# Values of the context in five blocks, and six reorderings, in a fused attention and mixture-of-experts kernel

## The chip, the cores and the metric

One Trainium2 chip, one core of it. The metric is the device time of one execution in microseconds (us). The kernel before takes 1630.91 us, the median of 3 runs (1629.7 to 1631.23). Engines: PE is the matrix engine (TensorE), DVE the vector engine, ACT the scalar engine, POOL the GpSimd engine; SP only issues DMAs. Each runs its own instruction stream in order and waits on semaphores.

## The reference

```python
def _L0_xattn_ref(queries, keys, values, Wq, bq, Wk, bk, Wv, bv, Wo, bo):   # 8 sequences, 512 rows, 77 context rows
    q = (queries @ Wq + bq).reshape(B, L, 16, 32)
    k = (keys @ Wk + bk).reshape(B, S, 16, 32)
    v = (values @ Wv + bv).reshape(B, S, 16, 32)
    scores = jnp.einsum('blhd,bshd->bhls', q, k)
    scores = jnp.where(causal[None, None], -jnp.inf, scores)      # triu, k=1
    attn = jax.nn.softmax(scores * scale, axis=-1)
    return jnp.einsum('bhls,bshd->blhd', attn, v).reshape(B, L, 512) @ Wo + bo

def _L0_ffn_ref(hidden_states, ...):      # attention runs over axis 0: the 8 sequences, causal, for each of 512 places
    ln1 = _layer_norm(hidden_states, ln1_weight, ln1_bias)
    ... q, k, v from ln1 @ qkv_weight.T (16 heads, 4 groups of keys), scores, softmax, proj ...
    h1 = hidden_states + proj
    x = _layer_norm(h1, ln2_weight, ln2_bias).reshape(-1, 512)
    probs = softmax(x @ router_weight)             # 8 experts, each token takes its best 2
    # each expert takes at most 1280 tokens, in order
    fc1 = jax.nn.gelu(jnp.einsum('ech,ehf->ecf', xt, moe_w1))
    fc2 = jnp.einsum('ecf,efh->ech', fc1, moe_w2)
    return h1 + (scatter-add of fc2 * padded_probs)
x = x + _L0_xattn_ref(_layernorm(x), ctx_1024, ctx_1024, ...)
x = x + _L0_ffn_ref(_layernorm(x), ...)
```

The 4096 rows are 32 tiles of 128. Weights and activations are float32; the large products are made as three passes of a high and a low half.

## The kernel before

There are two parts. The first (`build_main`) is a software pipeline of 52 steps written out by hand: in step i each engine does one stage of several tiles. With t a tile of the first attention and f a block of 128 tokens of the second, `tile(i, lag)` is the tile that is `lag` behind step i, and FF = 14 is where the second attention begins.

In step i PE does, in this order: the transposes of the normalized rows of tile i-1 ("xt"), the transposes of the probabilities of tile i-4 ("pt", four banks, L1010), those of the second attention ("p2t"), the transposes of z, the normalized block i-14 ("zt", L971, after waiting for `z_done`), in even steps the queries of two tiles (48 matmuls, L355), the output projection of tile i-5 ("wo", 12 matmuls), the second attention's scores and output ("s2", "o2"), the scores of tile i-2 ("s", L1060, into banks 0 to 3), the second attention's products (L1074) with the router's logits between them (L1079), for tiles 0 to 7 the values of one sequence ("val", L1091: 77 rows, 4 matmuls of 512 columns into bank 4 or 5), the transposes of the router's input ("z2t", L971 too), the product with the values of tile i-4 ("pv", L1103), the second projection ("pj"), and last, in steps 47 to 49 and 51, the prefix counts of the routing (`count_places`, L983 to L987).

DVE adds the causal mask to the scores of tiles 0 to 7 (L887), takes the row maximum (L888), subtracts it in two halves (L898), then adds the bias to the values (L918) straight into `va`, then forms the low halves of the attention's output (`oT_lo`, L821, wanted by wo) and of the transposed rows (`xT_lo`, L827, wanted by the queries), statistics, the sums of the exponentials (L952) and, last of a step, z (L959). In steps up to 14 ACT makes the exponentials of a tile in the next step, from then on in the same step; it normalizes x (`norm_x`, L563) before that in steps below 14 and after that from 14 on. POOL computes the factors of the normalizations, multiplies probabilities by their reciprocal sums (L482), and forms some low halves.

A PSUM bank is given out by `psum_plan`. Below step 14 each kind has banks of its own; from 14 on the jobs of a step take turns in banks 0 to 3 (half 0) and 4 to 7 (half 1), and a job waits until the readers of its bank's last user are done (`bank_free`). The scores always take banks 0 to 3. wo is in half 0.

The routing's choice of experts is made by `choose` on DVE: ten dependent small instructions for a batch of blocks, with 27 blocks in step 46, 4 in step 50 and the last one alone.

The second part (`build_experts`) goes over 8 experts by 5 groups of 256 tokens, 40 groups in all; a group whose first row is past the table has no tokens, and PE skips its matmuls. PE in a step: first layer of group i-6 (L1403, 96 matmuls), transposes of the gathered rows of group i-4 (L1416), second layer of group i-7 (L1432, 48 matmuls). POOL in a step: the gather of group i-3 (two indirect DMAs, L1292), the low halves of the next expert's weights (`low`, L1204), the scatter of group i-7 (two indirect DMAs, L1303). DVE makes `og`, the weighed result (L1372), which waits for the scatter of the group before; PE's second layer waits for `og` of the group before.

Of the kernel before, what the change touches and what calls it, by code (L numbers as in the profile page):

```python
# [18 lines left out]
ALU = mybir.AluOpType  # L19
# [147 lines left out]
CHOICES = ((STEPS - 6, 0, 27), (STEPS - 2, 27, 31), (STEPS, 31, 32))  # L167
COUNTS = {STEPS - 5: (0, 7, 1), STEPS - 4: (7, 15, 1), STEPS - 3: (15, 27, 1), STEPS - 1: (27, 31, 2)}
# [8 lines left out]
def psum_jobs(i):  # L177
# [8 lines left out]
    if tq is not None and tq < S:  # L186
        jobs += [("val", tq, 0, 1)]
# [4 lines left out]
def own_bank(kind, t, j):  # L192

    if kind == "q":
        return j
    if kind in ("pt", "val"):
        return 4 + j % 2
    odd = {"xt": t, "pv": t + LP - 1, "wo": t + LP + 1}[kind] % 2
    return 6 + odd


def psum_plan():
# [11 lines left out]
    for i in range(STEPS):  # L214
# [3 lines left out]
        for kind, t, j, half in psum_jobs(i):  # L218
            if i < FF and kind != "s":
# [9 lines left out]
def build_main(nc, a, x2d, mid, out2d, z2d, small, logits, tops, choice, row_table, weights, groups, sb, sem):  # L229
# [49 lines left out]
    bv = vbd[0:SK, :, :, :].rearrange("p g j d -> p (g j d)")  # L279
# [11 lines left out]
    gap, ex = sb("gap", [P, 1]), sb("ex", [P, 2])  # L291
# [6 lines left out]
    with main_psum:  # L298
# [18 lines left out]
        const_in = sem("const_in")  # L317
        place, ousted = psum_plan()
# [42 lines left out]

        def weight_piece(i):
# [19 lines left out]
        def _(sp):  # L382
# [19 lines left out]
            for i in range(STEPS):  # L402
                if 0 < i < NT - 2:
                    load_x(i + 2)
                t = tile(i, LP)
# [20 lines left out]
                if f is not None:  # L426
                    for n in range(2):
                        sp.wait_ge(x2_out[n], 16 * 4 * (f // 8 + 1))
                    sp.wait_ge(s["piece_lo"], 8)
                    need(sp, base_out[f % FX], 64 * (f // FX))  # L430
# [16 lines left out]
        def _(pool):  # L447
# [28 lines left out]
            for i in range(STEPS):  # L476
# [26 lines left out]
                if f is not None:  # L503
                    pool.wait_ge(s["v_kept"], f + 1)
                    pool.wait_ge(s["val_done"], S)
# [7 lines left out]
                if t is not None:  # L513
                    pool.wait_ge(bias_in, 32)
                    pool.wait_ge(xc_in[t % 2], 16 * (t // 2 + 1))
                    pool.tensor_tensor(xc[:, t % 2, :], xc[:, t % 2, :], bo[:, :], ALU.add).then_inc(s["bias_x"], 1)
                t = tile(i, -1)
# [11 lines left out]
                if i <= LATE:  # L529
                    factors(i)  # L530
# [18 lines left out]
                if i == 11:  # L549
                    pool.wait_ge(s["val_mm"], S)  # L550
# [9 lines left out]
        def _(act):  # L560
# [29 lines left out]
            act.dma_start(bv, a["L0_xattn_bv"].partition_broadcast(SK)).then_inc(bias_in, 16)  # L590
            act.dma_start(bo[:, :], a["L0_xattn_bo"].partition_broadcast(P)).then_inc(bias_in, 16)
            for i in range(STEPS):
# [27 lines left out]
                f = tile(i, FF)  # L620
                if f is not None:
                    act.wait_ge(s["zt_mm"], f + 1)
                    act.wait_ge(s["val_mm"], S)
                    need(act, s["z_lo"], f)
                    for k in range(KT):
# [878 lines left out]
```

## Time and profile before

| | |
|---|---|
| median of 3 runs | 1630.91 us |
| the profiled execution's own time | 1629.14 us |
| its span, first to last instruction | 1627.3 us |
| PE busy | 1517.0 us, 93% |
| DVE busy | 919.9 us, 57% |
| POOL busy | 839.5 us, 52% |
| ACT busy | 712.0 us, 44% |
| mean granted clock of PE | 0.964 of full speed |

PE is busy for 93% of the span, so the 110 us in which it isn't, and those in which its clock is lowered, are where reordering can act; beside it, only less PE work helps. In the page's forty slices PE's digit is 8 or 9 nearly everywhere, with lows at slice 21 (5), the passage between the two parts, at slice 32 (7), and at the end (6). The granted clock has its lows at slices 20 and 21.

### The profile page before, as it was taken

How to read it: one execution, taken by the hardware profiler on the slowest of the kernel's cores; microseconds unless marked ns; L12 is line 12 of the kernel's file. 1: busy time of each engine (PE TensorE's matmuls, PEld its weight loads, DVE VectorE, ACT ScalarE, POOL GpSimd, SP SyncE). 2: the span in 40 equal slices, each digit the busy share in tenths (PEclk: the TensorE clock that was granted, in tenths of full speed). 3: DMA queues.
4: the chain of work that ended last, by engine and by line, in shares of the span. 5: the costliest groups of instructions: out<-in, count | busy, mean ns of one | idle time of the engine just before them, and what ended most of it. 6: DMA issues, size and time to landing. Idle time of an engine off the chain costs nothing. (4 is left out here: it accounts for less than half of the span.)

```text
span 1627.3 us, 31053 instructions
## 1 busy us (share of the span) xinstructions
PE 1517.0 (93%) x11103; PEld 1326.0 (81%) x11104; DVE 919.9 (57%) x1719; ACT 712.0 (44%) x1425; POOL 839.5 (52%) x953
## 2 busy tenths in 40 slices
PE   7899889999999999999858999999999789999986
PEld 5577778888888888788648897998999689999976
DVE  3657457777777767787665455432333744343361
ACT  2445445555555555466315344432333633343351
POOL 2444444666556655688544566632533846454242
PEclk9999889999999999999968999999999989999999
DMA  6112111122212112122223233433422523442121
GB/s 247 47 48 72 57 64 50 64 79 73 71 68 85 58 56 78 64 88 89 82 72 102 59 94 94 113 77 72 91 67 50 126 66 93 100 104 50 29 39 24
DMA packets 63595, 124.57 MB, mean 77 GB/s; under 512 B 13231, under 2 KB 13647, under 8 KB 62920
## 3 DMA queue, kind: packets, MB, share of 16 engines
q1 hardware_dynamic: 45184, 92.54, 17.3%
q0 software_dynamic: 17920, 29.31, 10.3%
q8 instruction: 108, 1.77, 0.5%
q10 hardware_dynamic: 328, 0.50, 0.1%
q14 instruction: 55, 0.45, 0.1%
HBM read 89.02 MB, written 46.27 MB: 83 GB/s over the span
## 5 line engine op out<-in xcount | busy, mean ns | idle before, releaser
L1403 PE MATMUL hidden_ps<-gT,w 128*128 128x256 f32 x2880 | 356.1, 286 | 9.2 <-issue 6.0
L1403 PEld LDWEIGHTS hidden_ps<-gT,w 128*128 128x128 f32 x2880 | 353.6, 193 | 13.2 <-issue 7.6
L1432 PE MATMUL expert_ps<-w,hT 128*128 128x512 f32 x1440 | 342.4, 398 | 8.1 <-DVE og L1372 8.1
L1432 PEld LDWEIGHTS expert_ps<-w,hT 128*128 128x128 f32 x1440 | 272.9, 191 | 66.1 <-DVE og L1372 8.5
L1204 POOL TENSOR_TENSOR w<-raw,w 128x1024 fp32r<-128x1024 f32 x64 | 155.0, 2434 | 248.0 <-ACT w L1198 247.9
L1347 DVE TENSOR_TENSOR hT<-gl,hT 128x512 fp32r<-128x512 f32 x160 | 130.5, 824 | 259.4 <-ACT hT L1322 259.4
L1320 ACT ACTIVATE gl<-hidden_ps 128x512 f32<-128x512 f32 x160 | 95.7, 598 | 342.3 <-PE hidden_ps L1403 320.2
L1303 POOL DMA_INDIRECT out_dram<-og,idx x80 | 129.7, 1621 | 107.6 <-DVE og L1372 79.6
L1372 DVE TENSOR_SCALAR og<-expert_ps,kept 128x512 f32<-128x512 f32 x80 | 59.1, 749 | 157.7 <-PE expert_ps L1432 157.3
L1330 ACT ACTIVATE gT<-yk 128x256 fp32r<-128x256 f32 x160 | 66.9, 418 | 125.3 <-DVE yk L1358 123.9
L1292 POOL DMA_INDIRECT xg<-normed_tokens,idx x80 | 91.5, 1144 | 48.0 <-POOL idx L1287 33.6
L1074 PE MATMUL main_ps<-wqkv_hi,zT 128*128 128x512 f32 x256 | 108.9, 441 | 2.5 <-DVE h L851 2.5
L1322 ACT ACTIVATE hT<-hidden_ps 128x512 fp32r<-128x512 f32 x160 | 95.3, 596 | 15.1 <-PE expert_ps L1432 15.1
L864 DVE TENSOR_TENSOR x<-main_ps,xc 128x512 f32<-128x512 f32 x32 | 22.1, 691 | 122.9 <-PE main_ps L355 122.9
L1358 DVE TENSOR_SCALAR yk<-gather_ps,small 128x256 f32<-128x256 f32 x160 | 83.1, 540 | 2.9
L482 POOL TENSOR_TENSOR pr<-pr,rec 128x616 f32<-128x616 f32 x64 | 77.5, 1232 | 2.0 <-DVE rec L953 1.8
L355 PE MATMUL main_ps<-xT_hi,wq_hi 128*128 128x256 f32 x256 | 75.4, 295 | 2.9 <-DVE xT_lo L827 2.9
L1010 PE MATMUL main_ps<-small,pr 128*77 128x128 f32 x512 | 67.8, 285 | 11.0 <-ACT pT L610 5.5
L610 ACT ACTIVATE pT<-main_ps 77x512 f32<-77x512 f32 x128 | 67.1, 593 | 18.2 <-PE main_ps L1010 18.1
L355 PE MATMUL main_ps<-xT_lo,wq_hi 128*128 128x256 f32 x256 | 73.5, 287 | 0.0
L355 PE MATMUL main_ps<-xT_hi,wq_lo 128*128 128x256 f32 x256 | 73.5, 287 | 0.0
L1010 PEld LDWEIGHTS main_ps<-small,pr 128*77 128x77 f32 x512 | 60.4, 155 | 15.8 <-issue 14.8
(179 smaller groups left out, 3121.1 us busy)
## 6 DMA issues: line engine op xcount, KB each, us to landing
raw<-L_ffn_moe_w_dram SPq DMA_DIRECT2D x64, 512.0 KB, 3.6
normed_tokens<-h SPq DMA_DIRECT2D x128, 65.0 KB
xa<-x_dram SPq DMA_DIRECT2D x32, 256.0 KB, 2.7
xc<-x_dram SPq DMA_DIRECT2D x32, 256.0 KB, 3.0
attended_rows<-x SPq DMA_DIRECT2D x32, 256.0 KB, 2.2
fx<-attended_rows SPq DMA_DIRECT2D x128, 64.0 KB
out_dram<-fx SPq DMA_DIRECT2D x128, 64.0 KB
fx<-qkv_rows_dram SPq DMA_DIRECT2D x1, 1536.0 KB, 6.8
```

The costliest lines, as they stand in the source:

```text
L355: last = pe.matmul(dst, lhs(l, k), rhs(r, k), start=k == 0 and n == 0, stop=k == KT - 1 and n == 2)
L1010: last = pe.transpose(bank("pt", tp, b)[0:SK, g * P:(g + 1) * P], pr[:, tp % 2, b, g, :], ident)
L1074: last = pe.matmul(bank("qkv", fq, 0), zT[fq % 2][l][:, k, :], wqkv[r][:, k, 0:D], start=k == 0 and n == 0, stop=k == KT - 1 and n == 2)
L1204: pool.tensor_tensor(weight_piece(p, 1, j), raw[:, j % 2, :], weight_piece(p, 0, j).bitcast(F32), ALU.subtract).then_inc(s["w_lo"], 1)
L1292: pool.indirect_dma_start(out=xg[:, g.s % 2, k, :], out_offset=None, in_=z2d[:, :], in_offset=rows(g, k), bounds_check=N - 1, oob_is_err=F ...
L1303: pool.indirect_dma_start(out=out2d[:, :], out_offset=rows(g, k), in_=og[:, k, :], in_offset=None, bounds_check=N - 1, oob_is_err=False, c ...
L1320: act.activation(gl[:, q % 2, :], pH[:, q, :], ACT.Gelu_apprx_tanh)
L1322: act.activation(hT[g.s % 2][0][:, 2 * q:2 * q + 2, :].rearrange("p f n -> p (f n)"), pH[:, q, :], ACT.Gelu_apprx_tanh).then_inc(s["gelu"], 1)
L1347: dve.tensor_tensor(o[1], gl[:, q % 2, :], o[0].bitcast(F32), ALU.subtract)\
L1358: dve.tensor_scalar(yk[:, k % 2, :].rearrange("p (b n) -> p b n", b=GB), pT[:, :, k * P:(k + 1) * P], ln2w[:, k:k + 1], ln2b[:, k:k + 1], ...
L1403: last = pe.matmul(pH[:, q, f * W:(f + 1) * W], w1[p][l][:, k, cols], xT[g.s % 2][r][:, k, :], start=k == 0 and n == 0, stop=k == KT - 1 a ...
L1432: last = pe.matmul(pY[:, k, :], hT[par][l][:, f, k * P:(k + 1) * P], w2[p][r][:, f, :], start=f == 0 and n == 0, stop=f == FT - 1 and n == 2)
```

## The change

Five blocks of values. All 616 context rows are taken as 5 blocks of 128 rows (the last has 104) instead of 8 sequences of 77. Block b is computed in step b+2, ahead of the scores, and gets its bias on DVE into a staging tile (`fx[6]`), ahead of the scores' mask and maximum; SP then moves its rows to their sequences in `va` by two or three DMAs.

Order in the first part. zt goes behind the queries on PE, and its copies go behind the copies of q on ACT; wo's bank comes from half 1 instead of half 0; step 14 still uses the kinds' own banks; ACT's `norm_x` stays early up to step 15; DVE makes z ahead of the exponentials' sums in steps 13 and 14, POOL its factors earlier up to step 14.

Routing. The first batch of the choice is split in three of 9 (steps 42, 44, 46); the counts are spread over steps 47 to 51 and stand ahead of the scores' place in PE's step; `gap` has two columns.

Experts. POOL's order becomes gather (i-3), scatter (i-8), low halves: each scatter now comes behind the next gather. PE's first layer waits for the gathered rows quarter by quarter.

```diff
-CHOICES = ((STEPS - 6, 0, 27), (STEPS - 2, 27, 31), (STEPS, 31, 32))
-COUNTS = {STEPS - 5: (0, 7, 1), STEPS - 4: (7, 15, 1), STEPS - 3: (15, 27, 1), STEPS - 1: (27, 31, 2)}
+VB = -(-S * SK // P)
+CHOICES = ((STEPS - 10, 0, 9), (STEPS - 8, 9, 18), (STEPS - 6, 18, 27), (STEPS - 2, 27, 31), (STEPS, 31, 32))
+COUNTS = {STEPS - 5: (0, 6, 1), STEPS - 4: (6, 13, 2), STEPS - 3: (13, 21, 3), STEPS - 2: (21, 27, 3),
+          STEPS - 1: (27, 31, 4)}
...
-    jobs = [("xt", tx, 0, 1)] + [("pt", tp, j, 0) for j in range(4)] + [("p2t", fo, 0, 0), ("zt", fz, 0, 0)]
+    jobs = [("xt", tx, 0, 1)] + [("pt", tp, j, 0) for j in range(4)] + [("p2t", fo, 0, 0)]
...
-    jobs += [("wo", tw, 0, 0), ("s2", fs, 0, 1), ("o2", fo, 0, 1), ("s", tq, 0, 0), ("qkv", fq, 0, 1),
+    jobs += [("zt", fz, 0, 0), ("wo", tw, 0, 1), ("s2", fs, 0, 1), ("o2", fo, 0, 1)]
+    if 0 <= i - 2 < VB:
+        jobs += [("val", i - 2, 0, 1)]
+    jobs += [("s", tq, 0, 0), ("qkv", fq, 0, 1),
...
-            if i < FF and kind != "s":
+            if i <= FF and kind != "s":
...
+                b = i - 3
+                if 0 <= b < VB:
+                    sp.wait_ge(s["val_done"], b + 1)
+                    for seq, row, key, n in value_rows(b):
+                        sp.dma_start(va[key:key + n, seq, :, :].rearrange("p h d -> p (h d)"), stage[row:row + n, :])\
+                          .then_inc(va_in[b], 16)
...
+                b = i - 2
+                if 0 <= b < VB:
+                    dve.wait_ge(s["val_mm"], b + 1)
+                    dve.wait_ge(bias_in, 32)
+                    if b > 0:
+                        dve.wait_ge(va_in[b - 1], 16 * len(value_rows(b - 1)))
+                    n = min(P, S * SK - P * b)
+                    dve.tensor_tensor(stage[0:n, :], bank("val", b)[0:n, :], bv[0:n, :], ALU.add)\
+                       .then_inc(s["val_done"], 1)
...
-                if t is not None and t > 1 and i < FF:
+                if t is not None and t > 1 and i < FF + 2:
                     norm_x(t)
...
-                if fz is not None:
-                    pe.wait_ge(s["z_done"], fz + 1)
-                    transposes("zt", fz, z).then_inc(s["zt_mm"], 1)
                 if i % 2 == 0 and tq is not None:
...
+                if fz is not None:
+                    pe.wait_ge(s["z_done"], fz + 1)
+                    transposes("zt", fz, z).then_inc(s["zt_mm"], 1)
...
+                if i in COUNTS:
+                    count_places(*COUNTS[i])
+                b = i - 2
+                if 0 <= b < VB:
+                    pe.wait_ge(wv_in, 16)
+                    bank_free(pe, "val", b)
+                    n = min(P, S * SK - P * b)
+                    for k in range(KT):
+                        last = pe.matmul(bank("val", b)[0:n, :], cT[:, k, P * b:P * b + n], rv[:, k, :],
+                                         start=k == 0, stop=k == KT - 1)
+                    last.then_inc(s["val_mm"], 1)
...
-                    need(pe, s["val_done"], min(tp + 1, S))
+                    if tp < S:
+                        for b in range(tp * SK // P, (tp * SK + SK - 1) // P + 1):
+                            pe.wait_ge(va_in[b], 16 * len(value_rows(b)))
...
-                for piece in split_pieces(c, i):
-                    low(pool, *piece)
-                g = At(c, i - 7, PER)
+                g = At(c, i - 8, PER)
                 if g.within(NG):
...
+                for piece in split_pieces(c, i):
+                    low(pool, *piece)
...
-                    pe.wait_ge(s["xt_lo"], g.count(KT, KT))
+                    pe.wait_ge(s["xt_lo"], g.count(KT, 1))
...
+                                    if q == 0 and f == 0:
+                                        pe.wait_ge(s["xt_lo"], g.count(KT, k + 1))
```

## Rows read from the trace of the kernel before

**Rows 1.** Busy time by stretch: PE, PEld, DVE, ACT, POOL, clock, DMA share, GB/s.
```profile
280.00:640.00 360.00, 359.72 (x3155) 313.84 (x3154) 266.62 (x522) 199.14 (x439) 219.08 (x335) 1.00 0.21 69
```

**Rows 2.** Timeline of PE, steps 4 to 6: start, us, instruction, [idle before <-releaser].
```profile
60.73 1.13 PE L1060 MATMUL main_ps<-kT,qT 32*128 32x77 f32 x32 [1.24 <-ACT qT L638]
...
73.83 3.66 PE L1091 MATMUL main_ps<-ctx_then_block 128*77 128x512 f32 x8
...
81.87 0.37 PE L355 MATMUL main_ps<-xT_hi,wq_hi 128*128 128x256 f32 x1
...
90.50 1.13 PE L1060 MATMUL main_ps<-kT,qT 32*128 32x77 f32 x32
```

**Rows 3.** Timeline of DVE, step 5.
```profile
73.96 1.45 DVE L887 TENSOR_TENSOR main_ps<-main_ps,small 128x1232 f32<-128x1232 f32 x1
...
78.35 0.68 DVE L918 TENSOR_TENSOR va<-main_ps,vbd 77x512 f32<-77x512 f32 x1
79.19 0.69 DVE L821 TENSOR_TENSOR oT_lo<-main_ps,oT_hi 128x512 fp32r<-128x512 f32 x1 [0.17 <-ACT oT_hi L586]
```

**Rows 4.** The DMA issues: count, KB each, median us from issue to landing.
```profile
attended_rows<-x SPq DMA_DIRECT2D x32, 256.0 KB, 2.2
...
xg<-normed_tokens,idx POOLq DMA_INDIRECT x80, 3.6
out_dram<-og,idx POOLq DMA_INDIRECT x80, 5.7
```

**Rows 5.** Timeline of PE, steps 13 to 16.
```profile
179.59 1.13 PE L1060 MATMUL main_ps<-kT,qT 32*128 32x77 f32 x32
...
183.91 3.00 PE L1010 MATMUL main_ps<-small,pr 128*77 128x128 f32 x16 [1.60 <-DVE pr L898]
191.16 1.11 PE L971 MATMUL main_ps<-small,ctx_then_block 128*128 128x128 f32 x4 [4.24 <-DVE ctx_then_block L959]
...
202.77 1.13 PE L1060 MATMUL main_ps<-kT,qT 32*128 32x77 f32 x32 [0.88 <-DVE x L864]
...
208.45 1.12 PE L971 MATMUL main_ps<-small,xa 128*128 128x128 f32 x4 [3.54 <-ACT xa L563]
...
216.82 1.13 PE L1060 MATMUL main_ps<-kT,qT 32*128 32x77 f32 x32 [1.09 <-DVE x L864]
...
229.51 0.58 PE L355 MATMUL main_ps<-xT_hi,wq_hi 128*128 128x256 f32 x1 [0.66 <-DVE xT_lo L827]
```

**Rows 6.** Timeline of DVE, step 13.
```profile
185.07 0.68 DVE L827 TENSOR_TENSOR xT_lo<-main_ps,xT_hi 128x512 fp32r<-128x512 f32 x1
```

**Rows 7.** Timeline of DVE, the choice in steps 46 and 50.
```profile
778.39 0.38 DVE L732 TENSOR_TENSOR equal<-logits,tops 128x216 f32<-128x216 f32 x1
...
781.77 2.00 DVE L735 TENSOR_TENSOR hot<-first,consts 128x216 f32<-128x216 f32 x1
...
823.05 0.18 DVE L732 TENSOR_TENSOR equal<-logits,tops 128x32 f32<-128x32 f32 x1
```

**Rows 8.** Timeline of PE, steps 46 to 50.
```profile
785.08 0.52 PE L1074 MATMUL main_ps<-wqkv_hi,zT 128*128 128x512 f32 x1 [2.48 <-DVE h L851]
...
801.26 0.66 PE L971 MATMUL main_ps<-small,h 128*128 128x128 f32 x4 [2.38 <-DVE h L906]
...
822.92 1.11 PE L971 MATMUL main_ps<-small,h 128*128 128x128 f32 x4 [2.55 <-DVE h L906]
...
827.05 1.04 PE L1079 MATMUL main_ps<-small,ctx_then_block 128*128 128x8 f32 x8
```

**Rows 9.** Timeline of PE at its longest wait among the experts.
```profile
1301.87 1.09 PE L1416 MATMUL gather_ps<-small,xg 128*128 128x128 f32 x4 [8.73 <-DMA xg<-normed_tokens,idx]
```

**Rows 10.** Timeline of POOL ahead of that wait.
```profile
1293.41 1.89 POOL L1303 DMA_INDIRECT out_dram<-og,idx  x1 [0.16 <-issue]
...
1298.24 1.09 POOL L1292 DMA_INDIRECT xg<-normed_tokens,idx  x1 [0.88 <-POOL idx L1287]
```

**Rows 11.** Timeline of DVE in the same stretch.
```profile
1299.47 1.41 DVE L1372 TENSOR_SCALAR og<-expert_ps,kept 128x512 f32<-128x512 f32 x2
```

More of the change, by code:

```diff
@@ L317, in build_main @@
         const_in = sem("const_in")
+        va_in = [sem(f"va_in{b}") for b in range(VB)]
         place, ousted = psum_plan()
@@ L360, in parts, with value_rows @@
             return ap.rearrange("p (k n) -> p k n", k=KT)
+        def value_rows(b):
+            found = []
+            for seq in range(S):
+                first, end = max(seq * SK, P * b), min((seq + 1) * SK, P * (b + 1))
+                if first < end:
+                    found.append((seq, first - P * b, first - seq * SK, end - first))
+            return found
         def weight_piece(i):
@@ L619, in _ @@
                     act.activation(p2T, parts(bank("p2t", f)), ACT.Copy).then_inc(s["p2t_evac"], 1)
[L620 to L625, printed above, removed]
-                        act.activation(y[:, k, :], bank("zt", f)[:, k * P:(k + 1) * P], ACT.Identity,
-                                       bias=ln1b[:, k:k + 1], scale=ln1w[:, k:k + 1]).then_inc(s["y_done"], 1)
-                    act.wait_ge(s["y_done"], 4 * f + 4)
-                    need(act, s["qkv_mm"], 2 * (f - 1))
-                    act.activation(zT[f % 2][0][:, :, :], y, ACT.Copy).then_inc(s["z_hi"], 1)
                 if i % 2 == 0 and tile(i, 2) is not None:
@@ L639, in _ @@
                                        ACT.Identity, bias=bq[:, m:m + 1]).then_inc(s["q_evac"], 1)
+                f = tile(i, FF)
+                if f is not None:
+                    act.wait_ge(s["zt_mm"], f + 1)
+                    act.wait_ge(s["val_mm"], VB)
+                    need(act, s["z_lo"], f)
+                    for k in range(KT):
+                        act.activation(y[:, k, :], bank("zt", f)[:, k * P:(k + 1) * P], ACT.Identity,
+                                       bias=ln1b[:, k:k + 1], scale=ln1w[:, k:k + 1]).then_inc(s["y_done"], 1)
+                    act.wait_ge(s["y_done"], 4 * f + 4)
+                    need(act, s["qkv_mm"], 2 * (f - 1))
+                    act.activation(zT[f % 2][0][:, :, :], y, ACT.Copy).then_inc(s["z_hi"], 1)
                 t = tile(i, 0)
-                if t is not None and t > 1 and i < FF:
+                if t is not None and t > 1 and i < FF + 2:
                     norm_x(t)
@@ L673, in _ @@
                 t = tile(i, 0)
-                if t is not None and i >= FF:
+                if t is not None and i >= FF + 2:
                     norm_x(t)
@@ L688, in _ @@
                     need(act, s["weighed"], f - 1)
[L689 removed]
+                    act.activation(ex[:, f % 2:f % 2 + 1], gap[:, f % 2:f % 2 + 1], ACT.Exp).then_inc(s["gap_exp"], 1)
                 piece = weight_piece(i)
@@ L1086, in _ @@
                                   lambda h, k: wqkv[h][:, k, D:QKV]).then_inc(s["qkv_mm"], 1)
-                if tq is not None and tq < S:
-                    pe.wait_ge(wv_in, 16)
-                    bank_free(pe, "val", tq)
-                    for k in range(KT):
-                        last = pe.matmul(bank("val", tq)[0:SK, :], cT[:, k, tq * SK:(tq + 1) * SK], rv[:, k, :],
-                                         start=k == 0, stop=k == KT - 1)
-                    last.then_inc(s["val_mm"], 1)
                 if ft is not None:
```

55 lines of the change are left out of this document (29 added, 26 removed).

## The prediction

> **What bounds the kernel now.** First the busy shares: PE works 93% of the span, the others 44 to 57%. Then the same by stretch. From 280 to 640 us PE is busy for 359.72 of 360 us [rows 1]: in the steady steps nothing but less PE work can help, and the change takes none away there. So the question is what it does in the four places where PE isn't full: the steps that make values (2 to 9, up to 138 us), the steps where the second attention starts (13 to 17), the last steps of the first part (46 to 51), and the short steps among the experts. For each I read the timeline of PE for its waits, and of the engine named as releaser for what it had been doing.
>
> **Values in five blocks.** The four matmuls of a step's values take 3.66 us, 3.6 without the overlap with what follows [rows 2]; their length goes by the 512 columns, not by 77 or 128 rows, so five steps cost what five of the eight did: 3 x 3.6 = 10.8 us less PE work. That is not the gain. Before, the values stand behind the scores and cover DVE's work on them. From the values' end (73.83 + 3.66 = 77.49) to the queries at 81.87 PE has 4.4 us of other work [rows 2]. DVE starts on the scores at 73.96, is through mask, maximum and subtraction at 78.35 (4.4 us), and then forms oT_lo (0.6 to the next start) and xT_lo (0.7) [rows 3, 6]. In the new order, with no values behind the scores, wo may start 4.4 + 0.7 + 0.1 = 5.2 us after the scores' end and the queries 5.8 us after it, while PE is ready after 4.4: it waits 0.8 us in an odd and 1.4 us in an even step. The mask is there for tiles 0 to 7, so this holds at the passages into steps 5 to 10: 3 x (0.8 + 1.4) = 6.6 us given back. (From step 10 on there is no mask, and the order there is as before.) At the start the values, now between queries and scores, fill the 1.24 us in which PE waits for the copy of q in step 4 [rows 2], and the bias comes off DVE's queue ahead of the subtraction (0.68 us [rows 3]), which frees the banks of the next transposes; I take 2.2 us for both (bounds 1.2 and 3.6, the cover of one values step). Term 1: -10.8 + 6.6 - 2.2 = -6.4 us; bounds -13 (all of it PE's) and -2.
>
> The added DMAs cost nothing in the sum. SP issues a block's two or three in the step after its bias; DMAs of rows land 2.2 us after issue, and the extremes of that view are 2.2 and 5.7 [rows 4]. Their first reader is the product with the values, last in a PE step of 10 to 18 us; the other is DVE's next bias, which waits behind the queries and wo (8.6 us [rows 2]) in an even step. Behind SP's new wait stand only the loads of xc, wanted a step later. With that cover gone, four blocks (all but the first) would cost 2.2 us each. The wider bias load is one DMA at the start.
>
> **Steps 13 to 17.** The scores of step 13 end at 180.7 [rows 5]. PE then waits for a bank (1.60) and for z (4.24), and starts the queries at 191.16 + 0.76 = 191.9 [rows 5]. With step 14 on its own banks and zt behind the queries, what ends last is xT_lo, 185.07 + 0.68 = 185.8 [rows 6]: 6.1 us gained. z goes 0.7 us behind that, long before the queries (5.7 us) are over. Queries and wo took 191.9 to 201.9 = 10.0 us here against 81.87 to 90.50 = 8.6 us in step 6 [rows 2, 5]: they ran after 5.8 us of waits, at a lowered clock for part of it, so with waits under 1 us I take 1.4 us as gained (bounds 0 and 1.4). The scores' wait of 0.88 for DVE x goes with wo's bank; so does that of 1.09 in step 15 [rows 5]. zt adds 4 transposes behind the queries, 0.6 us, where they stood in a stall's shadow; in step 16 once more. In step 15 the wait of 3.54 for ACT's normalization [rows 5] goes too, but I count nothing for it: wo there hangs on oT_lo, which DVE reaches after maximum, subtraction, statistics, sums and z, all behind the same scores. In step 16 it is the same: the queries come 229.51 - 217.95 = 11.6 us after the scores [rows 5] by DVE's queue, whichever way zt is put. Term 2: -6.1 - 1.4 - 0.9 - 1.1 + 0.6 + 0.6 = -8.3 us; bounds -13 and -4. From step 17 on, zero: q goes ahead of y on ACT, and the scores, which now wait for y too in even steps, come 5.7 us (wo, s2, o2) behind zt, while y takes about 2.5. POOL's low half of z comes later in even steps, but the queue behind it waits for o2 anyway.
>
> **Choice.** The batch of 27 blocks runs from 778.39 until DVE h can release PE at 785.08: ten instructions of 0.38 us on 216 elements, one of which took 2.00 [rows 7]. PE waits 2.48 us for it [rows 8]. On 32 elements one takes 0.18 us [rows 7]; for 72 I take 0.23, with the gap between two 2.7 us for a batch. In step 46 DVE is then 3.1 us earlier, and the wait and (an estimate, from step 14's) 1.3 us of lower clock behind it are gone: -3.8. In steps 42 and 44 2.7 us are added to DVE, which has some idle time but is followed closely by PE: bounds 0 and 2.7 for each, I take 0.9. Term 3: -3.8 + 1.8 = -2.0 us; bounds -3.8 and +1.6.
>
> The 2.00 us instruction runs while POOL forms a low half of a weight. [...] It speaks against this change: the added batches run in steps where POOL is busier. If each met one such hold of 1.6 us, the sum would be 3.2 us smaller, and the time some 1610.
>
> **Counts.** From 822.92 + 1.1 to 827.05 the counts of 12 blocks stand on PE between two links of the routing's chain: 3.0 us, 0.25 a block [rows 8]. Put ahead of the logits they fall into waits of 2.38 and 2.55 us [rows 8]. Gained: 7 x 0.25 = 1.7 us in step 47; nothing in step 48, whose successor hangs on DVE and POOL behind pj; 1.5 us before the last logits, where six blocks' counts and the copies of y2 (1.5 us) now run together. Filled waits should also keep the clock up: 1.5 us, between 0 and 3. Term 4: -4.7 us; bounds -6 and -2.
>
> **Experts.** The longest wait, 8.73 us, is for a gather [rows 9]. POOL is busy without a break ahead of it; the gather's issue at 1298.24 stands behind a scatter that began at 1293.41, two issues of 1.9 us [rows 10]. In the new order it is issued 3.8 us earlier. What is late next is the scatter, issued 4 us later: `og` at 1299.47 [rows 11] waits for it, landing up to 5.7 us after issue [rows 4], and the second layer for `og`. So of 3.8 us I take 2 (bounds 0 and 5, if one other wait shortens too). In full steps of 23 us both have room. The finer wait of the first layer gains nothing: those rows are two steps old. Term 5: -2 us.
>
> **Sum.** -6.4 - 8.3 - 2.0 - 4.7 - 2 = -23.4 us. The profiled execution took 1629.1 us, 1.8 above its span of 1627.3, and is itself 1.8 below the median of 1630.9; 1629.1 - 23.4 = 1605.7 us, and against the median 1607.5. I say 1607.
>
> **Rivals.**
> A. PE stays the bound where I see DVE take over. For it: PE's waits in steps 4 to 12 are under 1 us before. Against: the sum 4.4 + 0.7 + 0.7 above. It gives 6.6 us more: 1600. Chance 0.12.
> B. The staging tile becomes the wait: DVE's bias waits until the last block has left it, scores' work is queued behind it, and PE gets wo and queries later. For it: one tile, not two, and SP's wait in order. Against: 8.6 us of cover. Four blocks at 2.2 to 3.6 us: +9 to +14, 1616 to 1621. Chance 0.15.
> C. The reordering of zt moves a wait and ends none: DVE's queue sets steps 14 to 17 throughout. For it: steps 15 and 16 as read above. Against: xT_lo at 185.8. Term 2 falls to -1: 1614. Chance 0.10.
> D. Slower: the scatter, now behind the gather, gets onto PE's path through `og`. Each group that it hits costs up to 1298.24 - 1293.41 = 4.8 us; it decides from 23.4 / 4.8 = 5 of the 40 groups on. With ten hit: +48 - 21.4 = +27, 1658. Against: in full steps a scatter has about 8 us to land in before the next `og`. Chance 0.05.
> E. The rule on SBUF ports as above, 1610: 0.04. No change to speak of (within 0.2%, 3 us, about what this kernel's measurement can tell): 0.02.
>
> The forecast keeps 0.52. From 1597 to 1619 about 8 in 10 are held. Faster 0.93, within 0.2% 0.02, slower 0.05.
>
> **What would show it.** The profile after should have 40 records of value matmuls at about 18 us; waits of about 1 us before wo and the queries in steps 5 to 10, released by oT_lo and xT_lo; queries of step 14 some 12.5 us earlier than 191.9; step 280 to 640's equivalent still full; no wait of 2.5 us behind the choice, and new ones under 1 us after steps 42 and 44; the gather's wait down from 8.7 to about 5 us, followed by one for `og`. Wrong would be: waits released by a DMA of the values, or by a scatter in full steps, or holes in the steady steps.

## The result, and the profile after

The kernel after takes 1609.87 us, the median of 4 runs (1608.39 to 1610.8), against 1630.31 us for the kernel before on the same chip (4 runs): a ratio of 0.9873, 95% interval 0.9856 to 0.989, some 20 us less. The forecast was 1607, its range 1597 to 1619. The profiled execution took 1610.14 us with a span of 1608.3; the span of before was 1627.3, so the two traces have 19.0 us to explain. The total came out close; the terms behind it did not. The ratios of the experiments below are to the kernel before as it was measured again with them (13 to 28 runs, medians 1629.15 to 1629.42).

The page of the kernel after, busy time of PE and its granted clock in 40 slices:

```profile
PE 1503.3 (93%) x11079; PEld 1319.9 (82%) x11080; DVE 918.7 (57%) x1736; ACT 711.1 (44%) x1425; POOL 836.4 (52%) x953
...
PEclk9899999999999999999968999999999999999998
```

PE is busy for 13.7 us less, of which the three steps of values fewer are 10.8 (3 x 3.6; a block of 128 rows takes no longer than the 77 rows did, 592 ns a record on average against 600, and the one of 104 rows 592 too), and still for 93% of the span. The steady steps are as full as those of [rows 1]:

```profile
270.00:630.00 360.00, 360.00 (x3156) 314.00 (x3155) 266.64 (x522) 200.92 (x443) 220.47 (x337) 1.00 0.21 69
```

To see where the lead arises I take one instruction of each step or group in two traces (DVE's maximum of the scores, DVE's sum into h, DVE's copy of a group's shares) and subtract its starts. Lead over the trace of before, us:

| trace | first scores | scores step 4 | step 11 | step 14 | h, step 41 | h, step 46 | group 2 | group 15 | 16 | 23 | 26 |
|---|---|---|---|---|---|---|---|---|---|---|---|
| after | -1.96 | -1.09 | 3.12 | 10.96 | 10.43 | 6.09 | 9.94 | 10.12 | 13.25 | 13.27 | 20.62 |
| values alone | -2.18 | -1.46 | 2.66 | 2.68 | 3.47 | 1.93 | 2.83 | 2.82 | 5.84 | 5.86 | 10.14 |
| order alone | 1.35 | 2.10 | 2.16 | 10.03 | 8.95 | 7.39 | 8.68 | 8.89 | 8.28 | 8.29 | 8.74 |
| experts alone | 0.23 | 2.54 | 2.60 | 4.00 | 4.19 | 2.64 | 4.05 | 4.11 | 4.05 | 4.06 | 7.54 |
| one batch | -2.14 | -1.60 | 2.48 | 10.34 | 9.61 | 7.72 | 9.71 | 9.64 | 12.94 | 12.96 | 20.15 |
| odd steps | -0.96 | 0.20 | 4.32 | 12.16 | 12.04 | 11.03 | 14.72 | 15.09 | 18.52 | 18.54 | 25.63 |
| spread, odd | -0.33 | 4.23 | 7.77 | 15.63 | 16.58 | 14.76 | 18.73 | 19.18 | 22.65 | 22.66 | 27.40 |

(The lower rows are experiments, told below.) The table also shows the noise of one trace: "experts alone" runs the code of before up to step 51, and is yet 2.5 us ahead at step 4 and 1.5 us less so between steps 41 and 46. Such differences are read off only where several traces agree.

### The profile page after: what moved, and what is told of

Its sections match the earlier page's. It is cut to its first block and busy times, and to the rows that moved or that the text cites. A ratio compares the mean times of both kernels' runs of the same rounds, so it can differ in the third digit from the quotient of the medians.

```text
span 1608.3 us, 31118 instructions
## 1 busy us (share of the span) xinstructions
PE 1503.3 (93%) x11079; PEld 1319.9 (82%) x11080; DVE 918.7 (57%) x1736; ACT 711.1 (44%) x1425; POOL 836.4 (52%) x953
## 5 line engine op out<-in xcount | busy, mean ns | idle before, releaser
L1445 PEld LDWEIGHTS hidden_ps<-gT,w 128*128 128x128 f32 x2880 | 350.0, 192 | 9.4 <-ACT hT L1362 4.2
L1445 PE MATMUL hidden_ps<-gT,w 128*128 128x256 f32 x2880 | 352.2, 284 | 5.8 <-ACT hT L1362 3.4
L1387 DVE TENSOR_TENSOR hT<-gl,hT 128x512 fp32r<-128x512 f32 x160 | 126.7, 800 | 251.6 <-ACT hT L1362 251.6
L1332 POOL DMA_INDIRECT xg<-normed_tokens,idx x80 | 89.0, 1113 | 58.8 <-POOL idx L1327 30.5
L1403 DVE TENSOR_TENSOR gT<-yk,gT 128x256 fp32r<-128x256 f32 x160 | 67.3, 421 | 7.3 <-ACT gT L1370 4.1
```

What stands on the lines that cost most here:

```text
L1332: pool.indirect_dma_start(out=xg[:, g.s % 2, k, :], out_offset=None, in_=z2d[:, :], in_offset=rows(g, k), bounds_check=N - 1, oob_is_err=F ...
L1387: dve.tensor_tensor(o[1], gl[:, q % 2, :], o[0].bitcast(F32), ALU.subtract)\
L1445: last = pe.matmul(pH[:, q, f * W:(f + 1) * W], w1[p][l][:, k, cols], xT[g.s % 2][r][:, k, :], start=k == 0 and n == 0, stop=k == KT - 1 a ...
```

## The experiments

**The choice in one batch again.** The kernel after, with

```diff
-CHOICES = ((STEPS - 10, 0, 9), (STEPS - 8, 9, 18), (STEPS - 6, 18, 27), (STEPS - 2, 27, 31), (STEPS, 31, 32))
+CHOICES = ((STEPS - 6, 0, 27), (STEPS - 2, 27, 31), (STEPS, 31, 32))
...
```

The lines left out number the batches in `COUNTS` to match.

> The kernel after, but the choice of 27 blocks in one batch in step 46 again. Theory P (the prediction's term 3: the split gains 2.0 us): 1609.9 + 2.0 = 1612. Theory H (each of the two added batches in steps 42 and 44 loses more than it saves, since its L761 is held for 2.0 us by POOL's low half of a weight): in the two traces the lead of the kernel after, read at the start of DVE h, falls from 10.43 (step 41) to 2.94 us (step 45) and comes back to 6.28 by step 47, so the split costs 10.43 - 6.28 = 4.1 us and this kernel takes 1609.9 - 4.1 = 1605.8. H expects in the trace no added wait in steps 42 to 45 and one of about 2.5 us before the products of step 46.

Measured: 1607.04 us (4 runs, 1605.63 to 1609.13), ratio to before 0.9858 (0.9843 to 0.9873), 2.8 us below the kernel after, with intervals that overlap. So the split did not gain, and by the trace it costs, though less than H's 4.1: from step 41 to 46 this kernel's lead falls too, by 1.89 us, and that of after by 4.34. The difference, 2.45 us, is the split (one trace of each).

**The batches in odd steps.** The kernel after, with

```diff
-CHOICES = ((STEPS - 10, 0, 9), (STEPS - 8, 9, 18), ...
+CHOICES = ((STEPS - 9, 0, 9), (STEPS - 7, 9, 18), ...
```

> The kernel after, with the first two batches of 9 blocks in steps 43 and 45 instead of 42 and 44. POOL forms a low half of a weight (2.4 us) at the end of steps 41, 43 and 45, beside the batches of steps 42, 44 and 46, and none at the end of 42 and 44. Theory H (the hold is the cost): L761 takes 0.23 us in both batches, 2 x 2.0 us go, and since a batch of 2.7 us is then partly in DVE's idle time, 4 to 6 us in all: 1604 to 1606. Theory D (any 2.7 us more on DVE's queue before h costs its whole length, hold or no hold): 2 x 2.0 = 4.0 us go and 2 x 2.2 stay: 1605.9, with a lead that still falls by more than 2 us at each batch. Theory N (the hold has nothing to do with POOL): L761 stays at 2.2 us in one of the steps and the time at 1609.9.

Measured: 1607.06 us (4 runs, 1605.08 to 1608.13), ratio 0.9863 (0.9848 to 0.9878), span 1603.2. DVE and POOL beside the batch of step 42 in the kernel after:

```profile
724.92 0.23 DVE L760 TENSOR_REDUCE first<-equal 128x9 f32<-128x72 f32 x1
725.19 2.23 DVE L761 TENSOR_TENSOR hot<-first,consts 128x72 f32<-128x72 f32 x1
...
724.97 2.35 POOL L1244 TENSOR_TENSOR w<-raw,w 128x1024 fp32r<-128x1024 f32 x1
```

and DVE in the batch of step 43 of this kernel:

```profile
734.37 0.23 DVE L760 TENSOR_REDUCE first<-equal 128x9 f32<-128x72 f32 x1
734.63 0.23 DVE L761 TENSOR_TENSOR hot<-first,consts 128x72 f32<-128x72 f32 x1
```

The same instruction on the same 72 columns takes 2.23 us beside POOL's low half of a weight, ending 0.10 us after it, and 0.23 us where POOL forms none. Not every instruction of DVE is slower there: in the kernel before a reduction of one input (L734) runs inside such an instruction of POOL in 0.38 us, as it does at 779.22 with no low half beside it, and the next one, with two inputs, does not ([rows 7] has its 2.00 us; it ends 0.24 us after POOL's; at 779.63, with no low half beside it, it takes 0.38):

```profile
781.36 0.38 DVE L734 TENSOR_REDUCE first<-equal 128x27 f32<-128x216 f32 x1
...
781.11 2.42 POOL L1204 TENSOR_TENSOR w<-raw,w 128x1024 fp32r<-128x1024 f32 x1
```

Both added batches of the kernel after and of the next one, which has them in steps 42 and 44 too, met such a hold of 2.23 us; neither of this one did, nor of the two later kernels with odd steps. From step 41 to 46 the kernels with even steps lose 4.34 and 4.31 us of lead, those with odd steps 1.01, 1.49 and 1.82, so by the traces the hold is worth 2.5 to 3.3 us; the medians say 2.8, which the intervals alone would not settle. N is out. D expected 2.2 us to be left at each batch; 1.0 to 1.8 in all is left, about what before's own code loses here in the other traces (1.55), so the hold was the cost and not the batch.

**The values' block behind the scores.** The kernel after, with the block's four matmuls moved to before's place behind the products, and its bias behind the subtraction:

```diff
-    if 0 <= i - 2 < VB:
-        jobs += [("val", i - 2, 0, 1)]
     jobs += [("s", tq, 0, 0), ("qkv", fq, 0, 1),
              ("lg", fr, 0, 1), ("qkv", fq, 1, 1)]
+    if 0 <= i - 2 < VB:
+        jobs += [("val", i - 2, 0, 1)]
```

> The kernel after, but the five blocks of values stand behind the scores on PE, and their bias behind the subtraction on DVE, as the eight did before. Theory C (cover: PE waits for oT_lo and xT_lo since no values stand behind the scores): the waits of 0.65, 1.15 and 0.65 us at the passages into steps 5, 6 and 7 and the 1.5 us of lowered clock in step 6 go, -4.0 us; at the start the prediction's 2.2 us come back: 1609.9 - 1.8 = 1608. Theory A (those waits cost nothing that counts or come otherwise): only the start's +2.2: 1612. In both the waits into steps 8, 9 and 10 stay.

Measured: 1607.32 us, but from 1603.01 to 1610.91 in 4 runs; ratio 0.987 (0.9855 to 0.9885): not told apart from the kernel after. The trace shows what the median doesn't: the first scores have a lead of 1.12 us here. Nine traces without values ahead of the scores, before's own among them, lie between -0.33 and 1.35 there, the five with them between -0.96 and -2.18. The lowered clock of step 6 is in the traces: the kernel after has a granted clock of 0.81 from 81.5 to 90.5 us, behind the queries' wait of 1.15, this one 1.00 from 76 to 92 us, without that wait.

**The expert part alone**, then **POOL's order alone**, both on the kernel before. The second is only

```diff
-                for piece in split_pieces(c, i):
-                    low(pool, *piece)
-                g = At(c, i - 7, PER)
+                g = At(c, i - 8, PER)
...
+                for piece in split_pieces(c, i):
+                    low(pool, *piece)
```

> The kernel before, with the expert part of the change alone (gather, scatter, low halves in POOL's order, and the first layer waiting for its rows quarter by quarter). Theory T (the traces): the lead grows by 2.6 us at each of two passages where PE was idle for nothing the profile shows (1122 and 1318 us before), by 2.6 before the second layer behind the gather's wait, by 4.7 at the first layer after it, less 1.6 of lowered clock at the end: about 9.6 us, 1630.3 - 9.6 = 1620.7. Theory P (the prediction's term 5): 2 us, 1628.3; then the lead in the second part came from what the first part changed (phases of gathers and loads).

> The kernel before, with only POOL's order among the experts changed (gather, scatter of the group one older, low halves); the first layer waits for all its rows as before. Theory G: the whole gain of the expert part (3.6 us in the medians, 4.4 in the trace between groups 24 and 26) is the gather that no longer stands behind a scatter: 1629.2 - 3.6 = 1625.6, the wait before the gathered rows at 6.1 us by DVE yk instead of 8.7 by the DMA. Theory Q: the quarter waits give it: 1629.2 and a wait of 8.7 as before. In both, PE's idle time before the first layer for nothing the profile shows stays at 5 to 6 us in all.

Measured: 1625.53 us (9 runs, 1621.67 to 1627.93), ratio 0.9976 (0.9967 to 0.9986), and 1624.31 us (11 runs, 1622.79 to 1626.79), ratio 0.9976 (0.9966 to 0.9985): 3.9 us each by the ratio. So the gain is POOL's order, and the quarter waits give nothing that can be told. In the kernel after, PE at the gather and POOL ahead of it, against [rows 9, 10]:

```profile
1286.36 1.97 PE L1459 MATMUL gather_ps<-small,xg 128*128 128x128 f32 x8 [6.37 <-DVE yk L1398]
...
1281.49 1.10 POOL L1332 DMA_INDIRECT xg<-normed_tokens,idx  x1 [0.97 <-POOL idx L1327]
1282.90 1.40 POOL L1332 DMA_INDIRECT xg<-normed_tokens,idx  x1 [0.31 <-issue]
1284.60 1.71 POOL L1341 DMA_INDIRECT out_dram<-og,idx  x1 [0.30 <-issue]
```

The gather goes first, and the wait is 6.37 us instead of 8.73. It isn't followed by one for `og`: what ends it now is DVE's `yk`. But T was wrong on the rest: PE's idle time for nothing the profile shows stayed at 5.3 and 4.9 us (6.0 before), while the kernel after has 2.4. That gain had to come from elsewhere.

**The five blocks alone**, on the kernel before (its old order, choice, counts and experts):

```diff
+VB = -(-S * SK // P)
-    jobs += [("wo", tw, 0, 0), ("s2", fs, 0, 1), ("o2", fo, 0, 1), ("s", tq, 0, 0), ...
+    jobs += [("wo", tw, 0, 0), ("s2", fs, 0, 1), ("o2", fo, 0, 1)]
+    if 0 <= i - 2 < VB:
+        jobs += [("val", i - 2, 0, 1)]
```

> The kernel before, with the five blocks of values ahead of the scores, their staging and DMAs alone. Theory P (the prediction's term 1): 6.4 us, 1622.8. Theory S (the traces: three kernels with the values ahead of the scores start their first scores 1.0 to 2.1 us later than before, and are 2.5 to 4.3 us ahead at the scores of step 12; the place ahead of the scores costs 2 at the start instead of giving 2.2): 3.3 us, 1625.9. Theory L (PE's idle time among the experts for nothing the profile shows, 5.3 and 6.0 us before, 2.0 to 2.4 in all kernels with the first part of after, goes by the length of PE's program ahead of the loop, which has 12 matmuls fewer): those 3 us and the lower clock behind them, 2 us, come on top: 1621. L is told from P by the trace: 2 us in place of 6.

Measured: 1618.88 us (5 runs, 1616.07 to 1620.82), ratio 0.9933 (0.992 to 0.9947), 10.3 us by the medians. The first part has 2.66 us of it at step 11. The rest comes between groups 15 and 16 (3.02) and 23 and 26 (4.28), as L said. PE at the first of these places, in the kernel before and in the kernel after:

```profile
1110.88 11.25 PE L1432 MATMUL expert_ps<-w,hT 128*128 128x512 f32 x48
1122.85 0.86 PE L1403 MATMUL hidden_ps<-gT,w 128*128 128x256 f32 x5 [0.72 <-issue]
1125.62 12.54 PE L1403 MATMUL hidden_ps<-gT,w 128*128 128x256 f32 x91 [1.91 <-issue]
```

```profile
1100.76 11.25 PE L1475 MATMUL expert_ps<-w,hT 128*128 128x512 f32 x48
1113.15 11.75 PE L1445 MATMUL hidden_ps<-gT,w 128*128 128x256 f32 x96 [1.15 <-issue]
```

These are the places where PE jumps back to the start of the experts' loop (groups come in turns of 10). Before, it does 5 matmuls of the new turn, then stands still for 1.91 us, waiting for nothing that the profile shows, and runs on at a lowered clock (96 matmuls take 13.40 us busy against 11.75; the granted clock is 0.89 on average from 1122 to 1138 us, and 1.00 from 1113 to 1125 us in the kernel after).

**The same with 12 matmuls put back.** Into the kernel with the five blocks alone, ahead of the scores:

```diff
+AGAIN = {7: 4, 8: 4, 9: 4}
...
+                    for n in range(AGAIN.get(i, 0)):
+                        pe.matmul(ps[:, 0, 0:SK], qT[0:DH, 0, (tq % 2) * P:(tq % 2 + 1) * P],
+                                  kT[0:DH, 0, (tq % S) * SK:(tq % S + 1) * SK], start=True, stop=True)
```

> The five blocks alone (the kernel of the run before that gave 1618.88), with the first scores matmul of the tile issued four more times ahead of the scores in each of steps 7, 8 and 9: 12 short matmuls more, so that PE's program is as long ahead of the experts' loop as before. Theory L (the place of the loop's first instructions in PE's program decides whether PE runs out of instructions after a jump back): the gap of about 2 us behind the first 5 matmuls of a turn of the loop is there again at both passages, idle time for nothing the profile shows 5 to 6.5 us, and 7.3 us are lost again: 1618.9 + 7.3 + 0.5 for the 12 matmuls = 1626.7. Theory V (the gap went because of the values' own doing, its DMAs or phases): it stays away, 1619.4.

Measured: 1628.05 us (12 runs), ratio 0.9991 (0.9982 to 1.0), 9.2 us more than without them. PE at the same place:

```profile
1123.43 0.85 PE L1435 MATMUL hidden_ps<-gT,w 128*128 128x256 f32 x5 [0.87 <-issue]
1126.15 12.68 PE L1435 MATMUL hidden_ps<-gT,w 128*128 128x256 f32 x91 [1.87 <-issue]
```

The gap is back behind the same 5 matmuls, and with it the 7.3 us: between groups 15 and 16 0.24 is lost where 3.02 were won, and between 23 and 26 0.04 is won where 4.28 were. V is out. The 12 matmuls themselves cost more than the 0.5 us I had put: in the next run but one four of them take 0.9 us, and in this trace the lead at step 41 is 3.24 us smaller than without them (0.23 against 3.47).

**One and four matmuls more, in the kernel before.** The same lines in the kernel before, with `AGAIN = {9: 1}` and `{9: 4}`.

> The kernel before, with one scores matmul of step 9 issued twice. A float32 matmul is two records in the trace, a matmul of the experts one, so theory L expects the gap of about 2 us after the first 3 matmuls of a turn of the loop instead of the first 5, at both passages, and the same time as before, 1629.2. Theory V expects it after 5, as in four kernels so far with this program length.

> The kernel before, with four more scores matmuls in step 9 and nothing else. Theory L: the gap moves 8 matmuls forward, from 5 to ahead of the loop's start, and is gone: idle time for nothing the profile shows 2 to 3 us in all and the kernel FASTER by about 7.3 - 0.2 us with more work: 1622. Theory V: 1629.4, with the gap after 5 matmuls. If the gap is instead put off to the end of the jump (before the first matmul, as one longer wait of about 3 us), 1629 too, but with a wait of over 2 us before the first matmul of the turn.

Measured: 1630.21 us (10 runs), ratio 1.0001 (0.999 to 1.0013), and 1634.15 us (11 runs), ratio 1.0022 (1.0009 to 1.0034). PE with one matmul more, and with four:

```profile
1122.78 0.62 PE L1407 MATMUL hidden_ps<-gT,w 128*128 128x256 f32 x3 [1.49 <-issue]
1125.83 13.55 PE L1407 MATMUL hidden_ps<-gT,w 128*128 128x256 f32 x93 [2.43 <-issue]
```

```profile
1130.14 13.28 PE L1407 MATMUL hidden_ps<-gT,w 128*128 128x256 f32 x96 [4.32 <-issue]
```

In these traces a float32 matmul is two records: the four added to the kernel before are x8, the tile's 16 scores matmuls behind them x32, and PE has 11103 records in all before, 11105 with one more and 11111 with four. The 96 matmuls of the experts' first layer are x96, one each. So one more puts the gap two matmuls of the experts forward: it comes after 3 instead of 5, as L said. With four it does not vanish, and the 1622 us that L forecast are missed by 12: it falls together with the wait at the jump into one of 4.32 us (4.83 at the second place), the third reading that the expectation named, which had put 1629 for it. By the lead the two jumps cost 3.1 us more than before's. So the place moves with the number of instructions ahead, but moving it forward to the start of the turn makes it worse; 24 records further into the turn, where the five blocks put it, it is not seen at all.

The traces bear on what PE stands still for. Their DMA records have a queue q8 of kind "instruction", 108 blocks of 16 KB in each kernel. `--dma` for 1122 to 1125.62 us of the kernel before, from the jump to the end of the gap (packets, MB, their time as a share of 16 engines):

```profile
q8 instruction: 1, 0.02, 3.0%
```

That one block is under way from 1122.63 to 1124.39 us, and PE runs on at 1125.62. All twelve gaps behind 3 or 5 matmuls, in six kernels, end 1.2 to 1.4 us after such a block has landed (at the second place of before: landed 1319.85, PE at 1321.10); with four matmuls more PE starts 1.9 and 2.0 us after. The kernel after gets this block too, at 1114.58, 1.43 us behind the first matmul of the turn (0.5 to 2.0 us in the seven kernels with 12 float32 matmuls fewer). Those (11079 records of PE against 11103) would by my estimate want it only behind 5 + 24 = 29 matmuls of 0.12 us (11.75 / 96), 3.5 us into the turn, and by then it is there. The traces don't name the engine that a block is for; that these are PE's is inferred from the times.

**zt and the order alone**, on the kernel before (the first-part order of the change without blocks, choice, counts and experts):

```diff
-            if i < FF and kind != "s":
+            if i <= FF and kind != "s":
...
-                if t is not None and t > 1 and i < FF:
+                if t is not None and t > 1 and i < FF + 2:
```

> The kernel before, with zt behind the queries, wo's bank in the other half, step 14 in the kinds' own banks, z and the factors earlier and the normalization of x early up to step 15; eight sequences of values, old choice, counts and experts. Theory P (the prediction's term 2): 8.3 us, 1620.9. Theory C (rival C: only a wait is moved): 1 us, 1628.2. By the trace of after the lead grows from 3.1 to 11.0 us at the scores of step 14 and is 10.1 at step 18: 7.0 us, 1622.2. Theory L expects the idle time for nothing the profile shows among the experts to stay at 5 to 6 us, since PE has as many instructions as before.

Measured: 1622.23 us (5 runs, 1620.81 to 1624.28), ratio 0.9961 (0.9947 to 0.9975), 7.0 us by the medians. The lead grows by 7.9 us from step 11 to 14 and gives back 1.1 by step 18; the idle time for nothing the profile shows is 6.6 us. C is out.

**Behind the scores, batches in odd steps**, the two edits above in one kernel.

> The kernel after, with the five blocks of values behind the scores and the first two batches of the choice in steps 43 and 45. By the medians of the two changes done alone (2.8 and 2.5 us): 1604.6. By the traces, if the holds (3.0 us) and the start with the cover (5.1 us at the scores of step 12) are what counts: 1609.9 - 8.1 = 1601.8. If the two share their gain with the clock's run-to-run spread, 1607.

Measured: 1606.98 us (4 runs, 1604.62 to 1607.58), ratio 0.986 (0.9845 to 0.9875). Its lead at step 11 is 3.4 us where the kernel with the values behind alone had 8.2: those 5 us were that trace's luck, and the place of the blocks in steps 2 to 6 makes no difference that can be told.

**Blocks spread over steps 2 to 9, behind the scores, batches in odd steps.**

```diff
+VALUES = (2, 4, 5, 7, 9)
...
-    if 0 <= i - 2 < VB:
-        jobs += [("val", i - 2, 0, 1)]
+    if i in VALUES:
+        jobs += [("val", VALUES.index(i), 0, 1)]
```

> The kernel after, with the values' blocks in steps 2, 4, 5, 7 and 9, behind the scores, and the first two batches of the choice in steps 43 and 45. Against the kernel with the blocks in steps 2 to 6 behind the scores (1607.0) the passages into steps 8 and 10 are covered instead of those into 4 and 7; xT_lo's waits of 1.37 and 1.36 us there go, and one of 0.65 comes: 2 us, 1605, if cover is what decides (theory C). If DVE's own length of a step decides (theory D: a mask step has 4.4 us of DVE behind the scores and PE waits as much wherever the values stand), no change: 1607.

Measured: 1600.04 us (5 runs, 1599.26 to 1602.14), ratio 0.9818 (0.9803 to 0.9834): 29 us below before, and the only kernel whose interval lies clear below that of after. PE's waits by what ended them, in steps 4 to 12, in the kernel after and in this one (total us, times, longest):

```profile
PE main_ps L1046 <- ACT pT L636: 6.6, 8, 1.0
PE main_ps L362 <- DVE xT_lo L853: 4.2, 4, 1.4
PE main_ps L362 <- DVE oT_lo L847: 2.2, 3, 0.9
```

```profile
PE main_ps L1047 <- ACT pT L637: 5.9, 8, 1.0
PE main_ps L363 <- DVE oT_lo L848: 1.5, 2, 0.9
PE main_ps L363 <- DVE xT_lo L854: 0.3, 1, 0.3
```

With a block's 3.6 us behind the scores of steps 5, 7 and 9, xT_lo is there when PE comes to the queries: 3.9 of 4.2 us are gone (of 3.1, against the kernel of the run before, 2.8), and D with them. The granted clock is higher too; stretch 100 to 180 us in after and here (the last but two is the granted clock):

```profile
100.00:180.00 80.00, 71.54 (x816) 61.19 (x814) 56.23 (x89) 42.29 (x79) 39.73 (x48) 0.98 0.23 74
```

```profile
100.00:180.00 80.00, 73.61 (x801) 60.54 (x800) 55.92 (x88) 42.25 (x78) 36.54 (x48) 1.00 0.25 79
```

The expected 1605 was too high by 5 us. Against the kernel of the run before, this trace is 4.4 us ahead at step 11: it is 4.1 ahead at step 4, having done one block (3.6 us) fewer by then, and does that block later without losing it again. 1.6 us more come between steps 14 and 18. It is one trace, in a stretch where traces of the same code differed by 5 us above; the median is sure, where it comes from is not, and no run takes these apart.

## Why the prediction was right, and where it wasn't

**Term 1, values: -6.4 predicted, -3.1 in the trace (-2.7 alone).** The lost cover is as forecast:

```profile
68.22 0.47 PE L362 MATMUL main_ps<-wo_hi,oT_hi 128*128 128x512 f32 x1 [0.65 <-DVE oT_lo L847]
...
81.50 0.38 PE L362 MATMUL main_ps<-xT_hi,wq_hi 128*128 128x256 f32 x1 [1.15 <-DVE xT_lo L853]
...
111.33 0.39 PE L362 MATMUL main_ps<-xT_hi,wq_hi 128*128 128x256 f32 x1 [1.37 <-DVE xT_lo L853]
...
136.16 0.39 PE L362 MATMUL main_ps<-xT_hi,wq_hi 128*128 128x256 f32 x1 [1.36 <-DVE xT_lo L853]
```

In steps 5 to 10 those waits (0.65, 1.15, 0.65, 1.37, 0.86, 1.36) sum to 6.04 us against 6.6. The step that failed is the start. I had the values fill PE's 1.24 us before the first scores and took 2.2 us for it; in five traces out of five the first scores came later, by 1.0 to 2.2 us, since a block is 3.6 us long and only 1.24 of waiting was there, and by step 4 0.9 us of it was back. That is 1.1 us lost instead of 2.2 won. The DMAs of the blocks released no wait in PE or DVE: B did not happen. (I had read 2.2 and 5.7 us as the extremes of the view of the DMAs; those are 2.1 and 12.9, the latter a weight at the start. Nothing hung on it.)

**Term 2, steps 13 to 17: -8.3 predicted, -7.0.** PE in the kernel after, against [rows 5]:

```profile
182.70 0.39 PE L362 MATMUL main_ps<-xT_hi,wq_hi 128*128 128x256 f32 x1 [1.12 <-DVE xT_lo L853]
...
198.81 0.66 PE L1007 MATMUL main_ps<-small,ctx_then_block 128*128 128x128 f32 x4 [0.73 <-DVE ctx_then_block L864]
201.20 0.70 PE L362 MATMUL main_ps<-wo_hi,oT_hi 128*128 128x512 f32 x1 [1.73 <-DVE oT_lo L847]
...
218.41 0.58 PE L362 MATMUL main_ps<-xT_hi,wq_hi 128*128 128x256 f32 x1 [3.78 <-DVE xT_lo L853]
```

The queries of step 14 start 9.2 us earlier, 6.1 of them here and 3.1 from the steps ahead (I had said some 12.5), behind xT_lo with a wait of 1.12; queries, zt and wo follow, up to the scores, in 9.1 us (182.70 to 191.80, at a granted clock of 1.00) against 10.9 (191.9 to 202.8, at a granted clock of 0.85 up to 202): 7.85 us from step 11 to 14. In steps 15 to 17 DVE's queue sets the pace as read, and 0.9 us is given back.

**Term 3, choice: -2.0 predicted, +4.3 in the trace.** Of these, 1.55 us is chance: six of the seven other traces of kernels with before's choice in before's place lose 1.5 to 1.6 us between steps 41 and 46 (the seventh 0.4). In step 41 the trace of before met no hold; here the trace of before, and then that of the expert part alone:

```profile
723.22 0.70 DVE L711 BATCH_NORM_STATS2 bnf<-fx 128x6 f32<-128x512 f32 x1 [0.36 <-DMA fx<-attended_rows]
...
726.77 0.69 DVE L893 TENSOR_TENSOR aT_lo<-ctx_then_block,aT_hi 128x512 fp32r<-128x512 f32 x1 [0.70 <-ACT aT_hi L659]
```

```profile
719.49 0.69 DVE L711 BATCH_NORM_STATS2 bnf<-fx 128x6 f32<-128x512 f32 x1 [0.82 <-DMA fx<-attended_rows]
...
723.04 1.54 DVE L893 TENSOR_TENSOR aT_lo<-ctx_then_block,aT_hi 128x512 fp32r<-128x512 f32 x1 [0.70 <-ACT aT_hi L659]
```

A DMA that lands 0.46 us later shifts DVE against POOL, and this instruction takes 1.54 us instead of 0.69, the next (L906) 1.28 instead of 0.54. In the second trace POOL's L500 (from 722.76, 1.28 us) and L508 (from 724.00, 1.50 us) run beside the two; in that of before L500 starts at 727.48, as L893 ends. The remaining +2.8 us is rival E, that each added batch meets a long instruction beside POOL's low half as that of step 46 did, 2.00 us. Its own sum gives term 3 +1.2; I had put its chance at 0.04 though the rows showed the hold and the added batches stood in steps of the same kind. It was also priced too low, at 1.6 us for a hold, the difference of 2.00 and 0.38 for 216 columns; on 72 columns it is 2.23 against 0.23, 2.0 us. That E's time, 1610, is the measured one is chance: it has none of the other errors. The gain in step 46 (3.15 us, from 2.94 to 6.09) came as forecast, with a granted clock behind the choice of 1.00 (779 to 794 us) against 0.89 before (785 to 800); steps 42 and 44 cost 5.9 us beside the chance, not 1.8. The rule that E names is shown by no run. What the runs show is the time beside POOL's low half of a weight, 2.23 against 0.23 us on 72 columns and 2.00 against 0.38 on 216, and no hold in the odd steps.

**Term 4, counts: -4.7 predicted, -3.9 in the trace,** of which about 1.1 us is in other traces of before's code too (group 2 against step 46: 0.8 to 1.4 in six, but -2.5 in the seventh): some 2.8 are the edit's, in the lower half of the bounds. The granted clock from step 46's products to the last logits is 0.91 in after (779 to 820 us) and 0.85 before (785 to 830). No run has the counts alone, so this share is argued from the traces and not shown.

**Term 5, experts: -2 predicted, -3.9 by the ratio.** The gather went as described (3.1 us of it in the trace, between groups 23 and 26); the next wait was not `og` but `yk`, and was shorter than feared. D did not happen.

**What no term had: 7.4 us,** the gap after the jump back, twice. In the trace of before it stood as idle time for nothing the profile shows, 6.0 us in all; I did not look at it because no edit touched that code. The page barely hints at it: the granted clock is at 8 in slice 33, which holds the second place, but also the second layer behind the gather's wait of 8.73 us. (I had named slices 20 and 21 for the clock's lows; they are 21 and 22, and 33 is one more.) The 12 matmuls that term 1 removes shift the gap. The sum of the trace: 3.1 + 7.0 + 0.3 - 4.3 + 3.9 + 0.2 + 7.4 + 3.0 (gather: 7.35 - 4.28, less 0.1 lost again by the end) - 1.6 (the last second layer, 12.79 against 11.18 us) = 19.0. The 1.6 is chance again: behind the same wait of 2.56 us these 48 matmuls take 11.2 us in eight of the fourteen traces and 12.8 in six, the latter at a lower granted clock (0.89 in after from 1584 to 1600 us, 1.00 in before from 1604 to 1620).

So the total was right by luck. Terms 1 to 4 promised 11.7 us more than the trace shows (3.3, 1.3, 6.3 and 0.8), and the unseen 7.4, with the 1.0 that the experts gave more, made up for most of it.

## What to carry to other kernels

Before moving work on the vector engine, look at what POOL does at that moment: an instruction with two inputs beside POOL's low half of a weight lost 2.0 us (2.23 against 0.23), and a batch moved by one step did not. Filler work (here the values) did best where it covers a chain on another engine, one piece per gap, and not all at the beginning (1600.04 against 1606.98 us). And when an edit changes the length of a program ahead of a loop, look at the first instructions of each turn before crediting the edit, and at the blocks of instructions in the DMA records; repeat a run with padding to tell.

## What was not expected of the hardware

- After a jump back, PE stood still for 1.0 to 2.7 us at one fixed place of its program: behind 5 matmuls in four of the five kernels with as many matmuls as before; behind 3 in the fifth, the expert part alone, which has more waits, and with one float32 matmul (two records) more; in one piece of 4.3 and 4.8 us at the jump with four more; and in none of the seven with 12 fewer. It looks like a wait for instructions, and the DMA records bear that out: it ends 1.2 to 1.4 us after a block of 16 KB of the queue "instruction" has landed, twelve times out of twelve.
- Four float32 matmuls into the same 77 columns took 0.9 us (131.93 to 132.83), 0.22 us each, where 16 into different banks and rows take 1.13.
- Two executions of the same code differ by up to 2.5 us in the first 60 us of the span, and the runs of one kernel by up to 9 us (1626.59 to 1635.52 in 28 runs of before, 1603.01 to 1610.91 in four with the values behind): gains of 2 or 3 us were settled here only where several traces agree.
